# V's product and small PE steps placed by tile shape, three output products in quarters of 32 rows, and ten score stretches of three in an attention-plus-adapter kernel

## What is computed

```python
xn = layernorm(x)                                   # 16 x 512 x 256
q = (xn @ Wq.T + bq) * 0.25;  k, v = split(xn @ Wkv.T + bkv)      # k, v: 16 wide, shared by 16 heads
attn = softmax(q_heads @ k.T) @ v;  attn_out = attn @ Wo.T + bo   # 8192 query rows x 512 keys a sequence
logits = xn @ w_gate;  gates = one_hot(argmax) * 1.0
tokens = A @ B;  a = softmax(xn @ tokens.T / 16)    # 6 experts x 100
delta = ((a @ val) + xn) @ wd.T + wd_b, scaled;  y = log(sum(exp(delta) * gates))
out = x + attn_out + (xn + y)
```

## Time and profile before

| what | value |
|---|---|
| median of 3 runs | 894.55 us (894.02 to 895.84) |
| profiled execution, its own time | 893.1 us |
| its span | 891.3 us |
| PE matmul busy | 837.5 us, 94% |
| PE weight load busy | 276.6 us, 31% |
| DVE busy | 770.9 us, 86% |
| ACT busy | 687.0 us, 77% |
| POOL busy | 566.8 us, 64% |
| mean busy share of the DMA engines | q1: 38.5% |
| mean granted PE clock | 0.973 of full speed |

### The profile page before, as it was taken

One profiled execution on the slowest core, in us unless ns is written; L12 is line 12 of the kernel. 1 busy time (PEld: TensorE's weight loads), 2 busy tenths in 40 slices (PEclk: granted clock), 3 DMA queues, 4 the chain that ended last, 5 costly groups with the idle time before them and its releaser, 6 DMA issues.

```text
span 891.3 us, 18198 instructions
## 1 busy us (share of the span) xinstructions
PE 837.5 (94%) x6038; PEld 276.6 (31%) x6038; DVE 770.9 (86%) x1488; ACT 687.0 (77%) x1386; POOL 566.8 (64%) x754
## 2 busy tenths in 40 slices
PE   6679999999999999999999999999999999999987
PEld 4333223332323332332323233232333333232213
DVE  7688898989989898998989899898989899898926
ACT  2226888888888888888888878888887888888883
POOL 2874677676667767666677766667775766646321
PEclk7688999999999999999999999999999999999989
DMA  4413243634433443534444453443435345241112
GB/s 118 116 41 66 68 101 86 131 86 127 102 97 86 121 107 97 126 93 107 91 109 107 104 120 86 120 98 91 113 97 120 86 119 112 62 105 62 63 52 71
DMA packets 125076, 86.09 MB, mean 97 GB/s; under 512 B 57143, under 2 KB 109112, under 8 KB 124984
## 3 DMA queue, kind: packets, MB, share of 16 engines
q1 hardware_dynamic: 124504, 84.56, 38.5%
q10 hardware_dynamic: 480, 0.36, 0.1%
HBM read 39.30 MB, written 33.54 MB: 82 GB/s over the span
## 4 chain that ended last, share of the span: by engine, by line
PE 76%; DVE 14%; issue 4%; POOL 3%; ACT 2%; DMA 1%; DVEq 0%; POOLq 0%
PE pO L376 24%; PE pA L358 18%; PE pB L363 8%; DVE M L850 8%; PE pA L499 5%; PE pA L446 5%; PE pA L518 4%; PE pA L501 3%; PE pA L435 3%; PE pA L471 2%; PE pA L486 2%; ACT P L658 2%; DVE st L778 1%; PE pB L479 1%; DVE RL L863 1%
## 5 line engine op out<-in xcount | busy, mean ns | idle before, releaser
L850 DVE TENSOR_REDUCE M<-pA 128x1 f32<-128x512 f32 x1024 | 650.0, 681 | 80.3 <-PE pA L358 79.0
L658 ACT ACTIVATE P<-pB 128x512 f32<-128x512 f32 x1002 | 556.5, 605 | 124.8 <-PE pB L363 120.5
L358 PE MATMUL pA<-K,Q 48*128 48x512 f16 x1024 | 320.3, 388 | 27.0 <-DVE M L850 15.0
L363 PE MATMUL pB<-Q,K 50*128 50x512 f16 x1002 | 314.0, 385 | 0.3 <-DVE M L850 0.2
L376 PE MATMUL pO<-P,VK 128*32 128x512 f32 x2048 | 273.9, 607 | 2.0 <-ACT OTr L664 1.1
L358 PEld LDWEIGHTS pA<-K,Q 48*128 48x128 f16 x1024 | 67.8, 94 | 337.7 <-DVE M L850 273.7
L1005 POOL TENSOR_TENSOR Rs<-Rs,Cz 128x512 f32<-128x512 f32 x32 | 40.7, 1272 | 51.1 <-ACT Cz L646 49.0
L376 PEld LDWEIGHTS pO<-P,VK 128*32 128x32 f32 x2048 | 40.6, 108 | 96.7 <-issue 56.8
L998 POOL TENSOR_SCALAR Cz<-Cx 128x512 f32<-128x512 f32 x32 | 62.1, 1941 | 11.5 <-ACT Cx L640 11.5
L363 PEld LDWEIGHTS pB<-Q,K 50*128 50x128 f16 x1002 | 64.1, 94 | 7.4 <-ACT P L658 5.5
L963 POOL CAST Qp<-qf 128x512 f16<-128x512 f32 x31 | 18.9, 610 | 66.4 <-ACT qf L607 66.3
(11 more groups left out here) (170 smaller groups left out, 897.5 us busy)
## 6 DMA issues: line engine op xcount, KB each, us to landing
o_parts<-OTr SPq DMA_DIRECT2D x62, 256.0 KB, 2.2
X<-in_x SPq DMA_DIRECT2D x16, 512.0 KB, 3.9
q_pieces<-Qp SPq DMA_DIRECT2D x64, 128.0 KB
out<-OUT SPq DMA_DIRECT2D x32, 256.0 KB, 3.4
Op<-o_parts SPq DMA_DIRECT2D x31, 256.0 KB
Rb<-l_parts SPq DMA_DIRECT2D x31, 256.0 KB
Q<-q_pieces SPq DMA_DIRECT2D x30, 256.0 KB, 4.7
Q<-q_pieces SPq DMA_DIRECT2D x34, 128.0 KB, 4.6
```

The source lines that it names most:

```text
L358: e.matmul(bank1("ab", t)[:, :], Q16[r:r + 48, b % 3, h, 128 * s:128 * s + 128], K16[r:r + 48, b % 3, :], start=True, stop=True).then_inc( ...
L363: e.matmul(bankB(t)[:, :], K16[r:r + 50, b % 3, 128 * i:128 * i + 128], Q16[r:r + 50, b % 3, :, 32 * hh:32 * hh + 32], start=True, stop=Tr ...
L658: e.activation(P[:, u % PR, :], bankB(u + LB)[:, :], ACT.Exp, scale=alpha).then_inc(S("e"))
L850: e.tensor_reduce(M[:, t // 32 % 2, t % 2, t % 32 // 2:t % 32 // 2 + 1], bank1("ab", t)[:, :], AX, ALU.max, negate=True).then_inc(S("mx"))
```

## The change

Five things change, with no arithmetic changed in value:

- A table `STRETCH` sets the score pairs into 27 stretches a block, 17 of two slots and 10 of three, in place of 32 of two. After the last block they stay as they were.
- `PV_AT`: the `pv` steps 5, 7 and 13 of each block stand at slot 4k + 0.5 in place of 4k + 1, that is behind a stretch of three which starts at slot 4k - 2. What each waits for is the same.
- `vg` moves from ring `pB` to ring `pA`, right behind `pv` 4; `vt` right behind `q1`; `o0`, `o2`, `o3` right behind a `pv`, and each of their matmuls is issued as four of 32 columns in four column tiles; `o1` and the last sequence stay whole. `p` moves by one stretch, `d2` by four slots.
- `M2` is padded with 64 zero columns, so that `mt` has a stationary operand of 128 columns. The zeros are written once, on POOL.
- DVE's `gate` becomes five steps that are placed between the maxima.

```diff
-    "kd": -41.6, "vg": -45, "vge": -44.3, "q1": -41, "qe1": -39.4, "qs1": -38.2, "qw1": -35.6,
-    "vt": -37, "vte": -36.4, "gate": -34.8, "mask": -32.6, "mkd": -31.4,
+    "kd": -41.6, "vg": -46.9, "vge": -46.3, "q1": -41, "qe1": -39.4, "qs1": -38.2, "qw1": -35.6,
+    "vt": -40.9, "vte": -38.2, "gate0": -36.2, "gate1": -35.2, "gate2": -34.2, "gate3": -33.2, "gate4": -32.7,
...
+STRETCH = (0, 2, 4, 7, 10, 12, 14, 16, 18, 21, 24, 26, 29, 32, 34, 36, 39, 42, 44, 46, 48, 50, 53, 56, 58, 60, 62)
+PV_AT = {5: 0.5, 7: 0.5, 13: 0.5}
...
+    def stretch(n):
+        k = n % 64
+        first = max(m for m in STRETCH if m <= k) if n < NT else k - k % 4
+        return n - k + first + 0.02 * (k - first)
+
     for n in range(NT + LB):
-        put("ab", n - n % 2 + 0.02 * (n % 2) if n < NT else n - n % 4 + 0.02 * (n % 4), n)
+        put("ab", stretch(n), n)
...
     for v in range(NT // 4):
-        put("pv", 4 * (v + LV + (v + LV >= NT // 4)) + 1, v)
+        k = v + LV + (v + LV >= NT // 4)
+        put("pv", 4 * k + (PV_AT.get(k % 16, 1) if k < NT // 4 else 1), v)
...
-        M2 = sb("M2", [128, 2, 2, H], F16)
+        M2 = sb("M2", [128, 128], F16)
...
                         for part in range(parts):
                             for k, (wp, op) in enumerate(PIECES):
-                                mm = e.matmul(bankO(t, b), OnP[:, b % 2, part, op, 128 * t:128 * t + 128],
-                                              woP[:, wp, part, :], start=(part == 0 and k == 0), stop=(part == 1 and k == 2))
+                                for m in range(4) if t != 1 and b < NB - 1 else (None,):
+                                    to = slice(0, 128) if m is None else slice(32 * m, 32 * m + 32)
+                                    mm = e.matmul(bankO(t, b)[to, :], OnP[:, b % 2, part, op, 128 * t:128 * t + 128][:, to],
+                                                  woP[:, wp, part, :], start=(part == 0 and k == 0),
+                                                  stop=(part == 1 and k == 2))
```

More of the change, by code:

```diff
@@ L41 @@
     "residual": 10.2, "q0": -53, "qe0": -51.4, "qs0": -46.5, "qw0": -44, "uk": -49, "uke": -47.4, "ks": -44.2,
-    "kd": -41.6, "vg": -45, "vge": -44.3, "q1": -41, "qe1": -39.4, "qs1": -38.2, "qw1": -35.6,
-    "vt": -37, "vte": -36.4, "gate": -34.8, "mask": -32.6, "mkd": -31.4,
[2 rows of a table added]
+    "mask": -32.2, "mkd": -31.4,
     "qread": -25.8, "utm": -24.9, "s": -21,
-    "smax": -20.4, "sexp": -18.8, "ssum": -17.4, "snorm": -16.2, "p": -13, "pte": -12.4, "a": -5, "mm": -4.4,
+    "smax": -20.4, "sexp": -18.8, "ssum": -17.4, "snorm": -16.2, "p": -8.9, "pte": -8.3, "a": -5, "mm": -4.4,
     "d0": -1, "dexp0": -0.4, "d1": 3, "dexp1": 3.6, "guard0": 6.1, "dlog0": 12.2, "radd0": 15.9,
[3 rows of a table removed]
[3 rows of a table added]
 }
@@ L52 @@
     "q0": -57, "qe0": -56, "qs0": -55, "qw0": -54, "uk": -53, "uke": -52, "ks": -51, "kd": -50, "q1": -52, "qe1": -51,
-    "qs1": -50, "vg": -50, "vge": -50.5, "vt": -48, "vte": -47, "gate": -46, "mask": -45, "qw1": -40, "mkd": -39,
+    "qs1": -50, "vg": -50, "vge": -50.5, "vt": -48, "vte": -47, "gate0": -46, "gate1": -45.9, "gate2": -45.8, "gate3": -45.7, "gate4": -45.6, "mask": -45, "qw1": -40, "mkd": -39,
     "utm": -30, "s": 9, "smax": 9.6, "sexp": 10.2, "ssum": 10.8, "snorm": 11.4, "p": 17, "pte": 17.6, "a": 21, "mm": 21.6,
@@ L89 @@
 DVE_NAMES = ("rngq", "rng", "two", "scl", "wl", "scd", "stats0", "stats1", "stats2", "stats3", "aggr", "refine", "xl0", "xl1",
-             "qs0", "gate", "smax", "ssum", "mm", "mx", "rec", "fo0", "fo1", "fo2",
+             "qs0", "gate0", "gate1", "gate2", "gate3", "gate4", "smax", "ssum", "mm", "mx", "rec", "fo0", "fo1", "fo2",
              "fo3", "nl00", "nl01", "nl02", "nl03", "nl10", "nl11", "nl12", "nl13")
@@ L265, in build @@
         ld = nc.dram_tensor("l_parts", (4, 8 * T), F32, kind="Internal").ap()
+        M2v = M2[:, 0:64].rearrange("p (a k h) -> p a k h", a=2, k=2)
         def bc(ap, n):
@@ L283, in build @@
             "uk": lambda b: (S("uke"), b + 1), "q0": lambda b: (S("qe0"), b + 1), "q1": lambda b: (S("qe1"), b + 1),
-            "a": lambda b: (S("mm"), b + 1), "rg": lambda b: (S("two"), 2), "bs": lambda b: (S("scl"), 1),
+            "a": lambda b: (S("mm"), b + 1), "vg": lambda b: (S("vge"), b + 1), "rg": lambda b: (S("two"), 2), "bs": lambda b: (S("scl"), 1),
             "o0": lambda b: (S("fo"), 4 * b + 1), "o1": lambda b: (S("fo"), 4 * b + 2),
@@ L291, in build @@
         FREED2 = {
-            "ab": lambda t: (S("e"), t - LB + 1), "vg": lambda b: (S("vge"), b + 1),
+            "ab": lambda t: (S("e"), t - LB + 1),
             "vt": lambda b: (S("gt"), b + 1), "p": lambda b: (S("pte"), b + 1),
@@ L450, in _ @@
                 if (b := due("vg", n)) is not None:
-                    w.wait_ge(*before2("vg", b))
+                    w.wait_ge(*before1("vg", b))
                     w.wait_ge(*turned(b))
@@ L456, in _ @@
                             for i in range(4):
-                                mm = e.matmul(bank2("vg", b)[32 * i:32 * i + 32, 0:128], wcP[:, wp, c, V0:V0 + 32],
+                                mm = e.matmul(bank1("vg", b)[32 * i:32 * i + 32, 0:128], wcP[:, wp, c, V0:V0 + 32],
                                               xT[:, b % 2, i, xp, c, :], start=(k == 0 and c == 0), stop=(k == 2 and c == 1))
@@ L506, in _ @@
                     w.wait_ge(S("m2"), g + 1)
-                    e.transpose(bank2("mt", g)[:, :].bitcast(F16)[0:64, 0:128],
-                                M2[:, :, :, :].rearrange("p a k h -> p (a k h)"), idh[:, :]).then_inc(S("mt"))
+                    w.wait_ge(S("mz"), 1)
+                    e.transpose(bank2("mt", g)[:, :].bitcast(F16)[:, 0:128], M2[:, :], idh[:, :]).then_inc(S("mt"))
                 for t in range(4):
@@ L613, in _ @@
                     w.wait_ge(S("vt"), b)
-                    e.activation(VGs[:, :], bank2("vg", b)[:, 0:128], ACT.Identity,
+                    e.activation(VGs[:, :], bank1("vg", b)[:, 0:128], ACT.Identity,
                                  scale=vsc[:, 0:1], bias=vgb[:, 0:1]).then_inc(S("vge"))
@@ L807, in _ @@
                     e.tensor_tensor(Qp[:, 0, 1, :], qf[:, 0, :], Qp[:, 0, 0, :], ALU.subtract).then_inc(S("ql0"))
-                if (b := due("gate", n)) is not None:
+                if (b := due("gate0", n)) is not None:
                     w.wait_ge(S("gt"), b + 1)
                     e.tensor_reduce(gmx[:, :], G[:, :, :], AX, ALU.max).then_inc(S("g0"))
+                if (b := due("gate1", n)) is not None:
                     w.wait_ge(S("g0"), b + 1)
                     e.tensor_tensor(geq[:, :, :], G[:, :, :], bc(gmx[:, :], NE), ALU.is_equal).then_inc(S("g1"))
+                if (b := due("gate2", n)) is not None:
                     w.wait_ge(S("g1"), b + 1)
@@ L817, in _ @@
                                     ALU.mult).then_inc(S("g2"))
+                if (b := due("gate3", n)) is not None:
                     w.wait_ge(S("g2"), b + 1)
                     e.tensor_reduce(gm2[:, :], gw[:, :, :], AX, ALU.max).then_inc(S("g3"))
+                if (b := due("gate4", n)) is not None:
                     w.wait_ge(S("g3"), b + 1)
@@ L882, in _ @@
             e.memset(mk[:, :, ER:128], 1.0).then_inc(S("mk1"))
+            e.memset(M2[:, 64:128], 0.0).then_inc(S("mz"))
             w.wait_ge(S("id"), 2)
@@ L984, in _ @@
                     w.wait_ge(S("ms"), g + 1)
[L985 removed]
+                    e.tensor_copy(M2v[:, :, 0, :], Ms[:, :, :]).then_inc(S("m1"))
                     w.wait_ge(S("m1"), g + 1)
[L987 removed]
+                    e.tensor_tensor(M2v[:, :, 1, :], Ms[:, :, :], M2v[:, :, 0, :], ALU.subtract).then_inc(S("m2"))
                 if (b := due("snorm", n)) is not None:
```

## The result

The changed kernel takes **943.28 us** (median of 4 runs, 943.18 to 944.35), the kernel before 894.28 in the same comparison: ratio **1.0549, interval 1.0531 to 1.0568**, slower. The forecast was 941 us with 929 to 965. The profiled execution took 943.2 us, 50.1 more than the one before.

The account below looks back on a forecast made before the run. PE, working in order, was taken to bound the kernel. Per block 3.6 us saved and 6.65 added, 3.05 us more; 14 blocks make 42.7, block 15 adds 2.5, block 0 adds 1: 893.1 becomes 939.3, the median 941 us, range 929 to 965.

Parts of the forecast that it names:

- `pv` 5, 7, 13 behind their own stretch: Each needs its stretch's second exponential, so starts 1.60 us after the stretch, not 0.76: 2.5 us a block, 0.1 more for `vge`.
- `pv` 2, 10 (needs the first of three): Each needs the first exponential of the stretch of three ahead, starting at 1.11 us, not 0.76: 0.7 us a block added.
- third pair behind each `mt`: This pair takes `mt`'s bank and waits for ACT's copy, starting at 1.40 us, not 1.06: 0.7 us a block added.
- slot 26 on `vt`'s bank: The pair of slot 26 waits until ACT's second copy of `vt` frees the bank: 1.0 us a block added.
- `pv` 8: It needs slot 31's exponential, behind ACT's `root` steps and copy of `pO`: 1.0 us a block added.
- `p` and the pairs around it: `p` needs its stretch's first pair's bank, the second pair behind it the third's: 0.65 us a block added.
- seams, turns, old waits: Savings on PE per block: five turns 0.45, seven seams of one shape 0.7, old waits removed; together 3.6 us.
- The rival by which seams of two types save nothing: Claimed float32 `pv` and float16 steps turn anyway: 0.4 us a block more, 947 us; no separate chance given.
- The clock falls too: Claimed the clock drops to 1.2 GHz around slot 26 to `pv` 7, costing 2.4 us each: 953 or 975 us; chance 0.33.
- The quarters load in the open: Claimed 24 weight loads stand in line in each of three output products: 3.1 us a block, 984 us; chance 0.03.
- The hidden waits win: Claimed ACT has exponentials done when PE is through, so removed waits win: 2 us a block faster, 866 us; chance 0.04.
- The sum for the ends: Added time outside the fourteen full blocks: about 2.5 us in block 15, 1 in block 0, tail unchanged.

Follow-up runs that it names:

- experiment 5: Kernel before with only the five gate steps on DVE placed between the maxima of slots 28 to 31: 889.81 us, ratio 0.9954.
- experiment 6: Changed kernel with the five gate steps on DVE in one go again: 942.39 us, ratio 1.054 to the kernel before.
- experiment 1: Changed kernel with the same shapes and merges, but stretches, `pv` and small steps laid out at other slots: 901.94 us, ratio 1.0061 to the kernel before.
- experiment 2: Changed kernel with only ACT's copies of `vt` placed earlier: 932.77 us, ratio 1.0413 to the kernel before.
- experiment 3: Changed kernel with stretches of two again and `pv` at its old slots, everything else kept: 914.12 us, ratio 1.0221 to the kernel before.
- experiment 7: Changed kernel laid out anew with stretches of three where DVE has few other steps, `o1` in quarters instead of `o2`: 872.99 us, ratio 0.9761 to the kernel before.
- experiment 8: Kernel of experiment 7 with `pv` 12 moved from behind slot 49 to behind slot 47, `o2` along: 899.93 us, ratio 1.0059 to the kernel before.
- experiment 9: Kernel of experiment 7 with transpose `p` moved to the other ring, of four banks: 874.41 us, ratio 0.9777 to the kernel before.
- experiment 4: Changed kernel with output products `o0`, `o2`, `o3` in whole matmuls of 128 columns again: 946.55 us, ratio 1.0574 to the kernel before.

## Why the prediction was right

**The mechanism and its price held.** The sum had +6.65 of new waits and -3.6 of savings, +3.05 a block; the trace has +3.03. Term by term, expected and measured:

| term | expected, us a block | measured |
|---|---|---|
| `pv` 5, 7, 13 behind their own stretch | 2.6 | 0.96 + 0.82 + 0.83 = 2.6 |
| `pv` 2, 10 (needs the first of three) | 0.7 | 2 x (1.11 - 0.76) = 0.7 |
| third pair behind each `mt` | 0.7 | 2 x (1.13 - 0.76) = 0.74 |
| slot 26 on `vt`'s bank | 1.0 | 1.00 |
| `pv` 8 | 1.0 | 0.84 |
| `p` and the pairs around it | 0.65 | 0.35 + 0.4, from another releaser |
| seams, turns, old waits | -3.6 | -3.6, what is left of 3.03 |

The last line is a remainder, not a measurement. Its parts that can be read: a seam without a turn saves 0.116 at `pv` (0.882 against 0.998), 0.095 at `q1` to `vt` (1.306 against 1.401) and at `d` to `mt` (0.435 against 0.530); I took 0.10 throughout. The rival by which seams of two types save nothing falls with that. One part of it had the wrong owner. The sum took 0.7 off at `o1` for the split gate and added 1.0 at `pv` 8, as if these were two things. In the kernel before the split gives 0.43 (experiment 5), and in the changed kernel it gives nothing (experiment 6), since the wait for `pv` 8's exponential takes the place of the one for DVE. The net of the two, +0.15 from `o1` to `pv` 8 (2.14 against 1.99), came out near the sum's 0.3 all the same.

**The rivals.** *The clock falls too* came true in a mild form: at the place named, in 3 blocks of 16, for 3.4 us and at 1.0 us each, where I had 6.8 us and 2.4. It adds about 3 of the 50 us, so the forecast at full clock stood nearer the result than 953. Between 100 and 825 us the profiled executions of experiments 1, 2, 3, 5, 7, 8 and 9 have no fall, that of experiment 4 has two and that of experiment 6 four; the first of these lasts 6.8 us in both. *The quarters load in the open* fell: a product of 24 matmuls holds PE 0.77, a whole one 0.76. The records of its 24 weight loads (PEld) lie beside those of matmuls: four beside `pv`'s, from 500.04, and twenty beside its own, which start at 500.47:

```profile
500.47 0.55 PEld L532 LDWEIGHTS pA<-woP,OnP 128*32 128x32 f16 x20 [0.31 <-issue]
```

With that the rule of the Trainium skill cited for it ("TensorE: Matmul & The Clock Gate", "The mechanism") is not borne out by column tiles that share their row groups.

*The hidden waits win* was wrong as the change stands, yet its number, 866, is near what the same shapes reach in other places: 873 in experiment 7.

**What was off.** The sum for the ends was 3.5 us (block 0 and block 15); against 14 x 3.03 = 42.4 the ends and the clock together make 7.7. Some 3 of that are the falls of the clock, and the remaining 1 us was not looked into. And I named as the wait at `p` a bank that ACT frees, where it was one that DVE's output step frees: `p` had moved next to an output product, and I had followed only its own ring.

That the total is within 2.3 us is in part luck: the sum added 1.45 for the median over the profiled execution, which is 0.06 here (943.28 against 943.2), and this covers part of the clock's 3. The period of 51.44 us stands twelve times in the trace before and not thirteen, and the waits of the rival with hidden waits add up to 3.3 and not 3.35; neither changes the forecast.

## What to carry to other kernels

A step that stands between a producer and its consumer on the bound engine may be all that hides the round trip: here 0.46 from pair to exponential, 0.60 for it and 0.49 for each one ahead in line. Before a step is moved or joined to another for its 0.1 us, look for each consumer behind it at how many steps ago its operand was issued, and at what else stands in the producer's queue. When such waits are gone, the next engine's bursts decide: experiments 1 and 7 have the same work in the same number of stretches, and differ by 1.57 us a block through where their steps stand. Since many steps moved between them, the share of each move is not shown.

## What the hardware showed that was not expected

- The granted clock can fall for a single stretch of 3.4 us in a steady block and be back, at a cost of 1.0 us; the fall in the tail of the kernel before lasted 6.8. It came at the same place of a block each time, but in three blocks only, though the records there are alike in the next block.
- A seam without a turn of shape saves PE about the same, 0.095 to 0.116 us, whether float32 goes into float16 (`pv` to an output product, `d` to `mt`) or float16 into float32 (`q1` to `vt`).
- A product in 24 quarter-wide matmuls takes only 0.01 us longer than in six, with four times as many weight loads.
